# Macaron block on one core: low halves of the gated columns in the shared feed-forward, made by GpSimd or by VectorE

## The reference

```
x = x + 0.5 * ffn(layernorm(x));  x = x + attn(layernorm(x));  x = x + 0.5 * ffn(layernorm(x))

def ffn(x):                                       # 16 experts, 512 hidden, plus one shared expert
    scores = softmax(x @ gate_w.T);  topk_w, topk_idx = top_k(scores over tokens, 256)
    x_tok = x[topk_idx]
    h = gelu(x_tok @ Wg.T) * (x_tok @ Wu.T)       # per expert
    out.at[topk_idx].add((h @ Wd.T) * topk_w)
    shared = (gelu(x @ Ws_g.T) * (x @ Ws_u.T)) @ Ws_d.T
    return out + shared
```

## Time and profile before

| | |
|---|---|
| time, median of 3 runs | 1587.62 us (1584.87 to 1591.28) |
| profiled execution: span from first to last instruction (no other time is given for it) | 1585.3 us |
| shared phase, first feed-forward | about 51 to 215 us of the span |
| shared phase, second feed-forward | about 1144 to 1307 us |
| granted TensorE clock over the span | 0.986 |

### The profile page before, as it was taken

How to read it: one execution, slowest core, us unless ns; L and a number is a source line. 1 busy time by engine, 2 the same in 40 slices (tenths; PEclk the granted TensorE clock), 3 DMA queues, 4 the chain that set the end, 5 groups by cost and what they waited for, 6 DMA issues and landing times. The chain is left out here.

```text
span 1585.3 us, 26702 instructions
## 1 busy us (share of the span) xinstructions
PE 1505.8 (95%) x10037; PEld 1050.0 (66%) x10037; DVE 889.6 (56%) x1961; ACT 982.7 (62%) x1332; POOL 553.3 (35%) x478
## 2 busy tenths in 40 slices
PE   4899999999997979999999999999799999999997
PEld 3788889888986863333333333333688888988896
DVE  6788667666755961113044332122788857766673
ACT  7422254455444869999999999998532235444542
POOL 3000245666544971112121122120300035566644
PEclk9999999999998989999999999999899999999999
DMA  7231256666645699404246353120413136666653
GB/s 275 74 98 50 65 159 154 151 155 155 147 80 153 236 280 176 74 10 82 36 87 104 99 83 62 21 67 27 171 37 106 50 112 156 156 150 155 151 123 40
DMA packets 121377, 181.05 MB, mean 114 GB/s; under 512 B 19040, under 2 KB 83040, under 8 KB 118496
## 3 DMA queue, kind: packets, MB, share of 16 engines
q1 hardware_dynamic: 92784, 130.56, 31.8%
q0 software_dynamic: 28464, 48.78, 15.0%
HBM read 123.73 MB, written 55.57 MB: 113 GB/s over the span
## 5 line engine op out<-in xcount | busy, mean ns | idle before, releaser
L1998 ACT ACTIVATE 8257_pr<-8257_pS 128x1024 f32<-128x1024 f32 x448 | 421.7, 1078 | 12.5 <-PE 8257_pS L1919 11.3
L1949 PE MATMUL 8257_pO<-8257_pr,6356_vres 128*32 128x512 f32 x1792 | 239.3, 606 | 5.5 <-DVE 8257_tO L2023 3.0
L1919 PEld LDWEIGHTS 8257_pS<-sq_rows,sk_rows 50*128 50x128 f32 x896 | 74.8, 185 | 202.5 <-ACT 8257_pr L1998 159.0
L1919 PE MATMUL 8257_pS<-sq_rows,sk_rows 50*128 50x512 f32 x896 | 186.2, 466 | 10.0 <-PEq L1551 5.5
L2023 DVE STREAM_TRANSPOSE 8257_tO<-8257_pO 128x512 f32<-128x512 f32 (+1 forms) x33 | 23.0, 699 | 258.1 <-PE 8257_pO L1949 255.3
L190 PE MATMUL 114_pGU<-columns_XT,weights_wts 128*128 128x512 f32 x384 | 152.7, 398 | 1.9 <-DVE columns_XT L956 1.6
L190 PE MATMUL 15224_pGU<-columns_XT,weights_wts 128*128 128x512 f32 x384 | 152.7, 398 | 1.8 <-DVE columns_XT L956 1.6
L191 PE MATMUL 114_pGU<-columns_XT,weights_wts 128*128 128x512 f32 x384 | 149.7, 390 | 0.0
L191 PE MATMUL 15224_pGU<-columns_XT,weights_wts 128*128 128x512 f32 x384 | 149.7, 390 | 0.0
L192 PE MATMUL 15224_pGU<-columns_XT,weights_wts 128*128 128x512 f32 x384 | 149.7, 390 | 0.0
L192 PE MATMUL 114_pGU<-columns_XT,weights_wts 128*128 128x512 f32 x384 | 149.7, 390 | 0.0
(11 more groups left out here) (392 smaller groups left out, 3419.1 us busy)
## 6 DMA issues: line engine op xcount, KB each, us to landing
114_raw_g<-WgT SPq DMA_DIRECT2D x16, 512.0 KB
114_raw_u<-WuT SPq DMA_DIRECT2D x16, 512.0 KB
114_raw_d<-WdT SPq DMA_DIRECT2D x16, 512.0 KB
q_rows<-rows_halves SPq DMA_DIRECT2D x8, 1024.0 KB, 5.1
k_rows<-rows_halves SPq DMA_DIRECT2D x8, 1024.0 KB, 5.1
15224_raw_g<-WgT SPq DMA_DIRECT2D x16, 512.0 KB
15224_raw_u<-WuT SPq DMA_DIRECT2D x16, 512.0 KB
15224_raw_d<-WdT SPq DMA_DIRECT2D x16, 512.0 KB
```

The lines of the kernel that those rows point to most:

```text
L1919: m = t_.matmul(to[:, e, :], key, query, start=True, stop=True)
L1949: m = t_.matmul(pO[e * 32:(e + 1) * 32, off:off + wd], vres[:, (g // GB) * TPB + kt, at:at + 32], from_(e), start=n == first[j], stop=n == ...
L1998: s_exp.done(a.activation(to, pS[:, u % RING, :, :], ACT.Exp, scale=HD ** -0.5))
```

## The change

Thirty of the 32 low halves of the shared phase (the units 0 to 29, `POOL_LOWS`) move from VectorE to GpSimd, with a semaphore of their own, `s_hlp`. The operation, its operands and its shape stay the same. Who waits for a low half (`mul` two units later, and the down product) now waits through `low_made`, which asks the one semaphore or the other. The units 30 and 31, and all of the expert phase, stay on VectorE. The lines of the changed kernel have numbers higher by 8 in the functions named here.

```
+            s_wls, s_hlp = sig("pool_wl"), sig("pool_hl")
+            POOL_LOWS = 4 * (J - 1) + 2
+            def low_made(eng, n):
+                if n <= POOL_LOWS:
+                    s_hlp.wait(eng, n)
+                else:
+                    s_hl.wait(eng, n - POOL_LOWS)
...
@@ down
-                        t_.wait_ge(*s_hl.at(4 * (d + 1)))
+                        low_made(t_, 4 * (d + 1))
...
@@ mul
-                    s_hl.wait(v, n - 1)
+                    low_made(v, n - 1)
...
@@ VectorE, shared loop
                     side(s, "d")
-                    low(s, 0)
-                    low(s, 1)
                     side(s, "e")
...
                     mul(s, 3)
-                    low(s, 2)
-                    low(s, 3)
                     if s <= 3:
                         split(J, s - 1)
...
@@ GpSimd
+                def low(n):
+                    s, f = n // 4 + 1, n % 4
+                    g.wait_ge(*s_hh.at(n + 1))
+                    s_hlp.done(g.tensor_tensor(hT[1][:, (s - 1) % 2, f, :], hf[:, f % 2, :],
+                                               hT[0][:, (s - 1) % 2, f, :].bitcast(f32), ALU.subtract))
+
+                for n in range(6):
+                    low(n)
                 for d in range(J):
+                    if 0 < d < J - 2:
+                        for n in range(4 * d + 2, 4 * d + 6):
+                            low(n)
                     g.wait_ge(*s_ev.at(2 * (d + 1)))
                     s_so[d % 2].done(g.dma_start(ov[d], eo[:, d % 2, :, :]))
                     if d == J - 3:
+                        for n in range(4 * d + 6, 4 * d + 10):
+                            low(n)
                         g.wait_ge(*s_idx.at(1))
```

More of the change, by code:

```diff
@@ L352, in ffn @@
                                             "dif", "cnt", "route", "go", "hot", "idx"))
-            s_wls = sig("pool_wl")
+            s_wls, s_hlp = sig("pool_wl"), sig("pool_hl")
[5 more added lines that the diff above has]
+                    s_hl.wait(eng, n - POOL_LOWS)
             s_Dq, s_evq = sig("pe_last_D"), sig("dve_last_ev")
@@ L675, in last_down @@
                 def last_down(d):
-                    t_.wait_ge(*s_hl.at(4 * d + FC - 1))
+                    low_made(t_, 4 * d + FC - 1)
                     s_wl.wait(t_, 3 * (d - J) + 3)
```

## The result

The changed kernel takes 1591.59 us in the median of 20 runs (fastest 1589.54). The kernel before, run beside it on the same chip, takes 1589.82 us. The ratio is 1.0017 with a 95% interval of 1.0009 to 1.0025, so the change costs about 2.7 us (1.4 to 4.0); the two medians by themselves lie 1.8 us apart. The forecast was a gain of 0.8 us. The profiled execution has a span of 1587.9 us, 2.6 us more than that of before.

The account below looks back on a forecast made before the run. TensorE was taken to bound the kernel. Per feed-forward, -0.96 + 0.28 - 0.52 + 0.27 + 0.5 = -0.4 us, -0.8 for both, so 1587.6 - 0.8 = 1586.8 us; range 1580.5 to 1594.5.

Parts of the forecast that it names:

- What bounds the kernel: Shared phases: TensorE sets the pace, busy 159.46 of 164 us; VectorE's 127 us matter only where TensorE waits.
- The hold of `cand`: At the counts: `cand`, with two SBUF inputs, waits for a running GpSimd subtraction to end, up to 1.28 us.
- count f of step 1: Without two subtractions on VectorE, `ge` ends before TensorE needs it: -0.96 us per feed-forward.
- step 2: Count b: weight split holds the fourth low half, which holds `cand`; TensorE resumes at 65.3, +0.28 us.
- steps 3 and 4: Count b: `ge` ends earlier despite the hold after the weight split, -0.26 us in each step.
- step 5: Count c: a low half of `mul` 0 can hold `cand` for 1.1 us, a new loss of +0.27 us.
- Masks and selection: Step 6: a low half pushes the first mask compare by 1.0 us; +0.3, and +0.2 at the later selection.
- As a queue this is harmless: GpSimd's 30 added subtractions, 38.5 us per feed-forward, are ready before their users need them; cost taken as nothing.
- The rival of the late low halves: Low halves reach `mul` or down product late, VectorE's one-hot series starving GpSimd; 1588.5 us at worst, 3%.
- my own rule: A VectorE operation with two SBUF inputs that comes during a GpSimd subtraction waits for its end, up to 1.28 us.
- The full relief: Rival: holds fall on `either`, not `cand`, so all four count waits go, 6.6 us, 1581.0 us; 12%.
- VectorE held at every low half: Rival: `cand` at counts c and d and compares of steps 6 to 8 held; +4 per feed-forward, 1595.6 us; 8%.

Follow-up runs that it names:

- e3: Changed kernel with VectorE's first token product moved from letter b to letter c of step 7, behind the next `mul`; 1587.25 us, ratio 0.999 to the kernel before.
- e5: Changed kernel with the first token product made as two halves of 2048 columns, at letters b and c of step 7; ratio 1.0018 to the kernel before.
- e12: The code of e5 measured again, beside the unaltered changed kernel on the same chip; ratio 1.0000 to the kernel before.
- e1: Changed kernel, but VectorE keeps the low halves of units 22 and 23 at their old place; 1585.29 us, ratio 0.9985 to the kernel before.
- e2: Changed kernel, but only the low halves of units 20 to 29 are on GpSimd; 1597.12 us, ratio 1.0048 to the kernel before.
- e10: Kernel of e2 with the first token product at letter c of step 7; ratio 1.0001 to the kernel before.
- e4: Kernel before, with low halves at f of step 1 and b of steps 2 to 4, and weight splits, placed behind those counts; 1584.6 us, ratio 0.9975.
- e9: Kernel of e1, units 3 and 16 also kept on VectorE, unit 3 and the weight splits behind the counts at b; 1583.68 us, ratio 0.9965.
- e6: Kernel before, with only the first token product moved from letter b to letter c of step 7; 1588.69 us, ratio 1.0006.
- e8: Changed kernel, VectorE keeping units 3, 7, 11, 16, 22, 23; units 3, 7, 11 and weight splits behind the counts at b; ratio 0.998.

## Why the prediction was wrong, point by point

- **What bounds the kernel** was right: TensorE paces the phase, and only its waits count.
- **The hold of `cand`** was right in place, and in size within 0.2 us: 1.06 us at b of steps 2 to 4, 1.23 at c of step 5. By the table, count f of step 1 gave -0.93 and -0.96 (forecast -0.96), step 2 gave +0.1 (+0.28), steps 3 and 4 between -0.14 and -0.40 (-0.26 each), step 5 +0.38 (+0.27). Masks and selection gave +0.03 and +0.05 (+0.5): TensorE had more in hand there than the one row told from which I took it. Together -0.4 per phase forecast for these, -1.1 and -1.0 measured; with nothing else, the kernel would have gained 2.1 us.
- **The step that failed** is the cost of the moved subtractions as a queue: "As a queue this is harmless", and with it "I cost all of that at nothing". It measured +2.4 us in each phase at the down product of step 7. The rival of the late low halves, at 3%, had the right place and one of the two long holders, but the wrong size: "VectorE's one-hot series in steps 6 and 7 could starve it for 2 us at most, and a unit has 2.7". Two things were missing. First, the token product, 2.29 us with two SBUF inputs, is by my own rule an operation that contends; I applied the rule only to VectorE's small steps as victims and never to its long ones as holders. Second, the slack was not 2.7 us, and the sentence "The down product comes later still" is wrong here. The down product at this place followed the last `mul` by 1.56 us and VectorE's low half by 0.16, which the timeline of before would have told; with nothing in its way, GpSimd's slower subtraction already makes that a wait of 0.4 (e3); half the product ahead of it makes 1.1 (e5 and e12), the whole product 2.2.
- **The experiments.** e1, e2, e3, e5 with e12, and e10 show this cause from five sides: without the two units, with little but them, with the product moved, halved, and moved again in e2. That the one-hot series adds 0.5 us of it, through the product's later end, is read from the timeline and was not tried by itself. e2's time is beyond what the cause explains, as said there, and only its wait counts here.
- **The other rivals.** The full relief did not come, since `cand` was held four times a phase. Nor was VectorE held at every low half: the median of `cand` stayed at 160 ns, and `either` paid more of it (493 ns in the mean instead of 155), as I had argued.
- **The signs.** "VectorE 41 us less busy" was wrong in itself: an instruction that is held counts as busy, so only 5 us show. GpSimd's 77 us more became 89 for the same reason. Long `cand` after the weight split, the wait gone at f, still there at b and new at c came as written, and so did the sign given for a wrong forecast, that the down product waits for GpSimd.

## What to carry to other kernels

When work goes from one of VectorE and GpSimd to the other, list for each engine not only the small operations that may be held, but the long ones that may hold: every long VectorE instruction with two SBUF inputs, every unbroken series like the one-hot compares, and which GpSimd instruction can fall into it. Slack is read at each user's own place in the timeline, not as a typical unit; an order on one engine that puts the urgent piece ahead of the long one is lost when the piece moves to another engine. And before moving work to relieve waits, try the order: e4 got 0.25% without GpSimd, e9 0.35% with 26 of 32 units moved and the others kept where they matter.

## What the runs showed of the hardware

- **The hold works both ways, and a series counts as one.** A VectorE operation with two SBUF inputs that comes during a GpSimd subtraction ends with it (`cand` 1.06 to 1.23 us for 0.16). In the changed kernel that held for all 8 `cand` and for 26 of the 27 `either` that began during a low half. Not held were the 12 `mul` (one input from PSUM, at most 0.69 us) and the 6 `drop` (at most 0.16) that began during one. A GpSimd subtraction that comes during such an operation ends 1.14 us after it (3.10 us for 1.28). The one-hot series of 16 separate instructions (16-bit, one input, 2.25 us) held GpSimd to its end as well: 2.58 us, although nine of the sixteen began after the low half did; the 14 shared phases of seven profiles show the same 2.57 to 2.58 us. The Trainium skill ("SBUF — State Buffer", section "Who interferes with whom") says that VectorE's two-port modes lock the shared ports for one whole instruction, and that whoever issues first wins. The trace agrees on the lock; that the compares run in such a mode is inferred from the hold. That a waiting GpSimd instruction gets no turn between the instructions of a series goes beyond what the page says. In the trace each compare begins 0.14 us after the one before and lasts about 0.21, so they overlap and the ports may never have come free; no run tells whether a gap between them would let GpSimd in.
- `ge`, the form with an accumulator, was never held: 745 to 749 ns in all 60, although 28 of them overlapped a low half of GpSimd and 4 began during one. The Trainium skill ("SBUF — State Buffer", section "Who interferes with whom") says that this form does not go for the shared ports, and the trace agrees.
- A pause of 2.2 us of TensorE was followed in three of six cases by 1.2 GHz instead of 2.4 for a while, at 1.5 us each, so that the wait cost up to 4.0 us; pauses of 1.1 us and less at the same place never were (eight cases). Nor was the pause of 1.6 us before the first expert item, in all 28 shared phases profiled. Whether the length of the pause decides or also what surrounds it, no run shows.
- The start-up differs between executions. The granted clock at 45 to 50 us of the span was 1.00 in seven of the profiles and 0.66 to 0.74 in the other seven (e2, e3, e6, e8, e9, e10, e12). Step 2 begins at 58.8 us in the changed kernel and at 62.5 in e3, whose code is the same up to there. Spans of single profiles are therefore no measure for effects of 1 or 2 us here; the table by steps, without step 1, is.
